# Reordering the instruction lists of five engines in a fused adaLN attention and feed-forward block on one core

## The chip, the cores and the metric

The kernel runs on one core of a Trainium2 chip. A core has five engines with an instruction list of their own: TensorE (PE, whose weight loads the profile shows as PEld), VectorE (DVE), ScalarE (ACT), GpSimd (POOL) and SyncE (SP, which here only issues transfers). An engine takes its list in order, and the lists meet only at semaphores. The metric is the device time of one execution in microseconds (us), as the median of several runs; one further execution was profiled.

## The reference

For each of 32 samples `x` is 256 rows of 128 numbers. What is computed, cut to what matters here:

```python
h = layernorm(x) * (1 + ca) + sa
Q, K, V = h @ wq, h @ wk, h @ wv                      # 16 heads of 8
local = window_attention(Q, K, V)                     # window 32, the block and the one before
GQ, GK, GV = h @ wgq, pool(h @ wgk), pool(h @ wgv)    # 8 heads, 64 latents, pooled over 4 rows
rem = softmax(mask(GQ @ GK.T / sqrt(8))) @ GV @ r_out_w
gl, gr = sigmoid(sum(Q * gate_local_w)), sigmoid(sum(Q * gate_remote_w))
x = x + ga * ((gl * local + gr * rem) @ w_out)
h = layernorm(x) * (1 + cb) + sb
x = x + gb * ffn(h)                                   # weights mixed per sample from the mean of relu(h @ w1.T + b1)
```

Everything is float32.

## The kernel before

**Stages.** After a set-up, 36 steps run the attention part as a software pipeline (`pipeline`), then four groups of eight samples run the feed-forward part. In step `it` five samples are in work at once: the first norm of sample `it`; projections, scores and softmax numerators of `it-1`; value products, gating and remote part of `it-2`; the output projection of `it-3`; the second norm and the hidden layer of the mixing gate of `it-4`. Steps 0 to 3 and 32 to 35 are written out, 4 to 31 are a hardware loop. Each engine has a `step(it)` that says in which order it takes the pieces; this order is written by hand, and it is what the change edits.

**Banks.** PSUM has eight banks: `SB[0..3]` hold the window scores of four head groups, then their transposed probabilities; `WB[0..3]` hold projections, latent scores, latent values, the gates, and the output products. `bank_free` makes TensorE wait until the last reader of a bank is done.

**One step, before the change.** TensorE: `projections` (wk and wq in L835 and L836, wgq and wgk in L839 and L840, wv in L847, the two gate products in L855 from `gate_w` and `hT`), `latent_T`, `probs_T` for all four groups (L896), `latent_values` (L946), `latent_value_rows` (L957), output projection (L987), transposes of the second norm (L994), `values` (L927, row sums in L931, into `SB[2]`), remote product (L1001), hidden layer (L1011, into `SB[1]`), transposes of the first norm (L1018), both `latent_scores` (L970), `scores` (L871 to L882). VectorE: both norms' statistics (L546, L551), `xn_a` (L555), latent denominators (`rlden` L615, `rem_n` L618), `GVBD` (L624), `y_ga` (L591), local denominators (`rden` L634, `a_loc` L636), pooling `hpT` (L640), the gating (L647, L649), then maxima and subtractions of the latent scores (L576, L582) and of the window scores (L561, L568). ScalarE: copies of `K_ch`, `QT`, `GQT`, `GKT`, `V_rows` (L411 to L426) with the exponentials of `probs` (L403) among them, `PL` (L435, L438), the four `PT` copies (L443), `xn_d` (L449), `h2T` (L452), relu (L456), `hT` (L464), exponentials of the latent scores (L470), tanh of the gates (L475). GpSimd: `KM` (L336, the keys spread over head groups), `inv_std` of the first norm (`ve_a` L327, `rstd_a` L329), the second norm's four small operations (L344 to L350), two halves of `PT_sum` (L358), `GKBD` (L364, the pooled keys spread over heads), `x_all` (L370), `attT` (L377). After steps 1, 2, 3 and 32 GpSimd also issues four expert-weight transfers (`load_experts`, L319 and L321). SyncE loads the next sample, stores `V_rows` and fetches it back as `VBD` when `pv_done` says that the last `VBD` has been read.

**Set-up of the gates.** After step 0 TensorE transposes wq (L1062), multiplies it by the gate columns (L1065), and ScalarE spreads the result into `gate_w` (L485); the gates are then products with `hT`.

The waits that set the order in the TensorE list look like this (L857 on, before the scores):

```python
pe.wait_ge(qt_ready, b + 1)
pe.wait_ge(km_ready, b + 1)
bank_free(pe, it, (0, hT_ready, 1, 1), (4, h2T_ready, 1, 1))
```

Of the kernel before, what the change touches and what calls it, by code (L numbers as in the profile page):

```python
# [13 lines left out]
P = 128  # L14
# [10 lines left out]
def adaln_block(nc, ins, out):  # L25
# [17 lines left out]
    with ExitStack() as ctx:  # L43
# [3 lines left out]
        def sem(name):  # L47
# [15 lines left out]
        tri, tri4, w_out, wqT, wv_in, gate_cols = (early[:, k, :] for k in range(6))  # L63
# [88 lines left out]
         silu_ready, siluT_done, siluT_ready, mod_done, mod_ready, ga_ready, ga_stored, ga_loaded, wqT_done,  # L152
         wqT_ready, attn_w_ready, gate_w_done, gate_w_ready, masks_ready, wT_done, wT_ready) = (sem(n) for n in (
             "mod_loaded", "attn_loaded", "w_loaded", "tw_loaded", "x_loaded", "mask_ready", "zeros_ready",
             "head_ready", "silu_exp", "silu_ready", "siluT_done", "siluT_ready", "mod_done", "mod_ready",
             "ga_ready", "ga_stored", "ga_loaded", "wqT_done", "wqT_ready", "attn_w_ready", "gate_w_done",
             "gate_w_ready", "masks_ready", "wT_done", "wT_ready"))
# [144 lines left out]
        def _(pool):  # L302
# [28 lines left out]
            def step(it):  # L331
# [6 lines left out]
                if has(it, 0):  # L338
                    inv_std(it, aggr_a, mv_a, ve_a, eps_a, rstd_a, rstd_a_s)
                if has(it, 4):  # L340
# [9 lines left out]
                    nc.gpsimd.tensor_tensor(shift_d[:], neg_d[:], rstd_d[:], ALU.mult).then_inc(shift_ready, 1)  # L350
                if has(it, 2):

                    b = it - 2
                    both = PT[:, 0:G * 2 * S].rearrange("p (g k s) -> p g k s", g=G, k=2)
                    for i in range(2):
                        pool.wait_ge(pt_copied, 4 * b + 2 * (i + 1))
                        pair = slice(2 * i, 2 * i + 2)
                        nc.gpsimd.tensor_tensor(PT_sum[:, pair, :], both[:, pair, 0, :], both[:, pair, 1, :], ALU.add  # L358
                                                ).then_inc(pts_ready, 1)
                if has(it, 1):  # L360

                    b = it - 1
                    pool.wait_ge(gq_ready, 2 * (b + 1))
                    nc.gpsimd.tensor_tensor(GKBD[0:NL], bc(GKT[:], [NL, LH, NL], 1),  # L364
                                            bc(head[0:NL, 0:LH], [NL, LH, NL], 2), ALU.mult).then_inc(gkbd_ready, 1)
# [29 lines left out]
        def _(act):  # L395
# [8 lines left out]

            def step(it):
                if has(it, 1):
# [4 lines left out]
                    nc.scalar.copy(K_ch[:], WB[0][:, S:2 * S]).then_inc(k_ready, 1)  # L411
                    nc.scalar.copy(QT[:], WB[0][:, 0:S]).then_inc(qt_ready, 1)
                if has(it, 2):
                    probs(it - 2, 1)
                if has(it, 1):
                    act.wait_ge(gqk_done, b + 1)
                    nc.scalar.activation(GQT[0:NL], WB[1][0:NL, 0:S], ACT.Copy, scale=SCALE / POOL).then_inc(gq_ready, 1)
                    nc.scalar.copy(GKT[:], WB[1][0:NL, S:S + NL]).then_inc(gq_ready, 1)
                if has(it, 2):
                    probs(it - 2, 2)  # L420
# [6 lines left out]
                if has(it, 2):  # L427
                    probs(it - 2, 3)
                if has(it, 2):
                    b = it - 2  # L430
                    if isinstance(it, int) and it == 2:
                        act.wait_ge(ga_stored, 16)

                    act.wait_ge(lpt_done, 2 * b + 1)
                    nc.scalar.copy(PL[:, :, 0:S].rearrange("p g (t s) -> p t g s", t=T),  # L435
                                   WB[0][:].rearrange("p (t g s) -> p t g s", t=T, g=LG)).then_inc(lpt_copied, 1)
                    act.wait_ge(lpt_done, 2 * b + 2)
                    nc.scalar.copy(PL[:, :, S:S + P],  # L438
                                   WB[1][:, 0:2 * P].rearrange("p (g s) -> p g s", g=LG)).then_inc(lpt_copied, 1)
                    for q in range(4):  # L440

                        act.wait_ge(pt_done, 4 * b + (q + 1))
                        nc.scalar.copy(PT[:, q * 2 * S:(q + 1) * 2 * S], SB[q][:]).then_inc(pt_copied, 1)  # L443
                if has(it, 4):
# [6 lines left out]
                    act.wait_ge(x2T_done, b + 1)  # L451
                    nc.scalar.activation(h2T[:, bass.ds(b * S, S)], SB[0][:, 0:S], ACT.Identity,  # L452
                                         scale=cb1T[:, bass.ds(b, 1)], bias=sbT[:, bass.ds(b, 1)]).then_inc(h2T_ready, 1)
                    act.wait_ge(hid_done, b + 1)

                    nc.scalar.activation(SB[1][:, 0:S], SB[1][:, 0:S], ACT.Relu, bias=gate_b1[:],  # L456
                                         accum_out=hsum[:, bass.ds(b, 1)]).then_inc(hid_summed, 1)
                if has(it, 0):
# [5 lines left out]
                    nc.scalar.activation(hT[:], SB[0][:, 0:S], ACT.Identity, scale=ca1T[:, bass.ds(it, 1)],  # L464
                                         bias=saT[:, bass.ds(it, 1)]).then_inc(hT_ready, 1)
                if has(it, 1):
                    b = it - 1
                    for t, pl in ((0, PlA), (1, PlB)):
                        act.wait_ge(ls_sub, 2 * b + (t + 1))
                        nc.scalar.activation(pl[:], pl[:], ACT.Exp).then_inc(pl_ready, 1)  # L470

# [5 lines left out]
                    probs(b, 0)  # L477

            def after(it):
                if it == 0:  # L480
                    act.wait_ge(wqT_done, 1)
                    nc.scalar.copy(wqT, SB[1][:, 0:D]).then_inc(wqT_ready, 1)
                    act.wait_ge(gate_w_done, 1)
                    for k in range(2):
                        nc.scalar.copy(gate_w[:, k, :].rearrange("p (h d) -> p h d", d=HD),  # L485
                                       bc(SB[2][:, k * H:(k + 1) * H], [P, H, HD], 2)).then_inc(gate_w_ready, 1)
# [24 lines left out]
        def _(dve):  # L511
# [83 lines left out]
            def step(it):  # L595
# [3 lines left out]
                if has(it, 0):  # L599
                    dve.wait_ge(x_loaded, 16 * (it + 1))  # L600
                    stats(x_all[:, bass.ds(it * S, S)], st_a, stat_a, mv_a, aggr_a, it)
# [3 lines left out]
                if has(it, 0):  # L605
                    dve.wait_ge(rstd_a_s, it + 1)
                    at_least(dve, xT_done, it)
                    normed(x_all[:, bass.ds(it * S, S)], mv_a, rstd_a, xn_a, xn_a_s)
                    if isinstance(it, int) and it == 0:
                        modulation()  # L610
# [8 lines left out]
                if has(it, 1):  # L619

# [7 lines left out]
                if has(it, 3) and not tail:  # L628
                    output_times_ga(it - 3)
                if has(it, 2):  # L630
# [3 lines left out]
                    nc.vector.reciprocal(rden[:], SB[2][:, S:2 * S]).then_inc(rden_ready, 1)  # L634
                    dve.wait_ge(rden_ready, b + 1)
                    nc.vector.tensor_tensor(a_loc[:], SB[2][:, 0:S], rden[:], ALU.mult).then_inc(a_ready, 1)  # L636
                if has(it, 0):

                    dve.wait_ge(hT_ready, it + 1)
                    nc.vector.tensor_reduce(hpT[:], hT[:].rearrange("p (n k) -> p n k", k=POOL), AX.X, ALU.add  # L640
                                            ).then_inc(hp_ready, 1)
                if has(it, 2):
                    b = it - 2
                    dve.wait_ge(a_ready, b + 1)
# [493 lines left out]
```

## Time and profile before

| what | us |
|---|---|
| median of 3 runs | 749.49 |
| lowest and highest run | 747.51, 749.99 |
| profiled execution, its device time | 748.97 |
| profiled execution, span from first to last instruction | 747.2 |
| busy in the span: PE, DVE, ACT, POOL | 645.6, 538.1, 384.9, 294.9 |
| granted TensorE clock, mean over the span | 0.979 |

The profiled execution took 748.97 us, 1.77 us more than its span and 0.52 us less than the median. In the timeline a row gives the start, the duration, the engine, the line, what is written from what, and in square brackets how long the engine had been idle and what ended that. Rows of the same group of instructions are merged, with their count. Step 2 begins with the projections at 34.86, step 32 at 524.93; the feed-forward groups fill the time from about 575.

### The profile page before, as it was taken

Reading aid. Unit: us, or ns where it says so; the run is one execution under the profiler, and the core shown is the slowest. Engines: PE = TensorE matmul, PEld = TensorE weight load, DVE = VectorE, ACT = ScalarE, POOL = GpSimd, SP = SyncE. Lnnn points to the kernel's source line nnn. Section 1 sums busy time; section 2 is a strip of 40 time slices with the busy share of each in tenths; the row PEclk is TensorE's granted clock in tenths of the full one; section 3 lists DMA queues with packets and bytes.
Section 4 is the critical chain, followed back from the end, with each engine's and each line's share of the span. In section 5 each row is a group of like instructions: output and inputs, shape, how many; then the busy total and the mean of one; then the engine's idle time right before and its main releaser. Section 6 shows DMA issues by size and latency. Waiting matters only on the chain.

```text
span 747.2 us, 24120 instructions
## 1 busy us (share of the span) xinstructions
PE 645.6 (86%) x8822; PEld 506.4 (68%) x8822; DVE 538.1 (72%) x1241; ACT 384.9 (52%) x910; POOL 294.9 (39%) x415
## 2 busy tenths in 40 slices
PE   5588888788888878888887888888779999999998
PEld 3366666566666656666665666666558999898996
DVE  5568788888878888887888888788755546273552
ACT  2256655666665566666555666655543223423233
POOL 2256555455555545555554555555530000000000
PEclk9699999999999999999999999999978999999999
DMA  3757111000101100010110001010140010100101
GB/s 99 174 78 96 32 24 32 21 21 21 28 22 24 31 21 21 21 28 21 24 32 21 21 21 28 21 24 18 29 44 0 10 35 15 32 24 21 34 9 49
DMA packets 65797, 24.84 MB, mean 33 GB/s; under 512 B 38440, under 2 KB 64360, under 8 KB 65648
## 3 DMA queue, kind: packets, MB, share of 16 engines
q1 hardware_dynamic: 64320, 18.25, 10.2%
q0 software_dynamic: 1456, 6.31, 5.6%
q8 instruction: 14, 0.23, 0.1%
q14 instruction: 7, 0.06, 0.0%
HBM read 16.13 MB, written 8.40 MB: 33 GB/s over the span
## 4 chain that ended last, share of the span: by engine, by line
PE 42%; DVE 26%; ACT 15%; issue 14%; POOL 1%; ACTq 1%; DVEq 1%; DMA 0%; SPq 0%; POOLq 0%
DVE mx L561 10%; PE SB L820 7%; PE WB L808 7%; DVE rden L634 5%; ACT PT L443 5%; PE SB L927 5%; PE WB L795 4%; PE SB L795 4%; ACT xn_d L449 4%; DVE Pr L568 3%; ACT Pr L403 3%; PE SB L882 2%; PE SB L931 2%; ACT PL L435 2%; PE WB L970 2%
## 5 line engine op out<-in xcount | busy, mean ns | idle before, releaser
L336 POOL TENSOR_TENSOR KM<-K_ch,bd_scale 128x1024 f32<-128x1024 f32 x32 | 60.6, 1893 | 125.2 <-ACT K_ch L411 125.2
L634 DVE RECIPROCAL rden<-SB 128x256 f32<-128x256 f32 x32 | 56.2, 1758 | 54.5 <-PE SB L931 54.5
L506 ACT ACTIVATE Pr<-WB,mb1T 128x256 f32<-128x256 f32 x128 | 49.8, 477 | 75.7 <-PE WB L808 75.6
L561 DVE TENSOR_REDUCE mx<-SB 128x8 f32<-128x512 f32 x128 | 87.2, 681 | 1.5 <-PE SB L882 1.5
L403 ACT ACTIVATE Pr<-Pr 128x512 f32<-128x512 f32 x128 | 80.8, 631 | 10.8 <-DVE Pr L568 7.2
L568 DVE TENSOR_TENSOR Pr<-SB,mx 128x512 f32<-128x512 f32 x128 | 84.6, 681 | 0.0
L358 POOL TENSOR_TENSOR PT_sum<-PT 128x512 f32<-128x512 f32 x64 | 80.3, 1275 | 3.8 <-ACT PT L443 3.8
L443 ACT COPY PT<-SB 128x512 f32<-128x512 f32 x128 | 66.1, 622 | 0.0
L896 PE MATMUL SB<-ident,Pr 128*128 128x128 f32 x512 | 63.0, 276 | 0.9 <-ACT Pr L403 0.9
L820 PE MATMUL SB<-Pr,GA 128*128 128x256 f32 x256 | 61.2, 381 | 0.0
L835 PE MATMUL WB<-hT,wk 128*128 128x256 f32 x64 | 23.3, 448 | 43.2 <-DVE PlB L582 43.2
L808 PE MATMUL WB<-h2T,mW 128*128 (+1 forms) x256 | 60.2, 380 | 0.0
L896 PEld LDWEIGHTS SB<-ident,Pr 128*128 128x128 f32 x512 | 57.8, 143 | 1.8 <-ACT Pr L403 1.8
L377 POOL TENSOR_TENSOR attT<-a_gated,rem_g 128x256 f32<-128x256 f32 x32 | 23.2, 725 | 88.8 <-DVE a_gated L647 85.7
L470 ACT ACTIVATE PlA<-PlA 128x256 f32<-128x256 f32 x32 | 13.3, 416 | 79.5 <-DVE PlA L582 79.5
L808 PEld LDWEIGHTS WB<-h2T,mW 128*128 128x128 f32 x256 | 48.2, 190 | 6.4
L820 PEld LDWEIGHTS SB<-Pr,GA 128*128 128x128 f32 x256 | 46.1, 190 | 6.2 <-DVE GA L675 1.2
L835 PEld LDWEIGHTS WB<-hT,wk 128*128 128x128 f32 x64 | 10.0, 196 | 57.7 <-DVE PlB L582 53.7
L882 PE MATMUL SB<-KM,QT 32*32 32x256 f32 x2048 | 48.4, 387 | 0.0
L970 PE MATMUL WB<-GKBD,GQT 128*128 128x512 f32 (+1 forms) x128 | 47.9, 498 | 0.0
L456 ACT ACTIVATE SB<-SB,gate_b 128x256 f32<-128x256 f32 x32 | 14.3, 448 | 63.8 <-PE SB L1011 63.8
L615 DVE RECIPROCAL rlden<-WB 128x128 f32<-128x128 f32 x32 | 30.7, 958 | 19.7 <-PE WB L946 19.7
(195 smaller groups left out, 1518.5 us busy)
## 6 DMA issues: line engine op xcount, KB each, us to landing
x_all<-in_L_attn_x SPq DMA_DIRECT2D x32, 128.0 KB, 2.1
v_rows<-V_rows SPq DMA_DIRECT2D x32, 128.0 KB, 1.8
VBD<-v_rows SPq DMA_DIRECT2D x128, 32.0 KB, 1.8
TW<-in_L_ffn_TW POOLq DMA_DIRECT2D x16, 256.0 KB, 9.5
GA<-ga_rows POOLq DMA_DIRECT2D x1, 2048.0 KB, 10.5
out_x<-attT SPq DMA_DIRECT2D x16, 128.0 KB, 1.8
out_x<-y_ga SPq DMA_DIRECT2D x16, 128.0 KB, 1.8
PT<-in_L_ffn_W SPq DMA_DIRECT2D x2, 256.0 KB
```

What stands on the lines that cost most here:

```text
L336: nc.gpsimd.tensor_tensor(KM[:, :, W:KW], bc(K_ch[:], [P, 4, S], 1), bc(bd_scale[:], [P, 4, S], 2), ALU.mult).then_inc(km_ready, 1)
L358: nc.gpsimd.tensor_tensor(PT_sum[:, pair, :], both[:, pair, 0, :], both[:, pair, 1, :], ALU.add).then_inc(pts_ready, 1)
L403: nc.scalar.activation(Pr[:, k, :], Pr[:, k, :], ACT.Exp).then_inc(p_ready, 1)
L443: nc.scalar.copy(PT[:, q * 2 * S:(q + 1) * 2 * S], SB[q][:]).then_inc(pt_copied, 1)
L561: nc.vector.tensor_reduce(mx[:, k, :], SB[k][:].rearrange("p (h j) -> p h j", h=8), AX.X, ALU.max).then_inc(mx_ready, 1)
L568: nc.vector.tensor_tensor(Pr[:, k, :].rearrange("p (w h c) -> p h w c", w=2, h=8), SB[k][:].rearrange("p (h w c) -> p h w c", w=2, h=8), b ...
L634: nc.vector.reciprocal(rden[:], SB[2][:, S:2 * S]).then_inc(rden_ready, 1)
L808: last = mm(WB[2 * (j % 2) + c // 2][:, (c % 2) * S:(c % 2 + 1) * S], mW1[:, j, c * P:(c + 1) * P], h2T[:, bass.ds((g * GB + j) * S, S)], ...
L820: last = mm(SB[j % 2][:, 0:S], mW2[:, c, j, :], u[j % 2][:, c, :], start=(c == 0), stop=(c == FC - 1))
L882: last = mm(SB[g][W * q:W * q + W, 4 * HALF * t:4 * HALF * (t + 1)].rearrange("p (h j) -> p h j", h=4), QT[rows, W * blk:W * blk + W], KM[ ...
L896: last = nc.tensor.transpose(SB[q][:, k * P:(k + 1) * P], Pr[:, q, o:o + P], ident[:])
L970: mm(WB[1 - t][:, 0:8 * m].rearrange("p (h j) -> p h j", h=8), GQT[:, t * P:(t + 1) * P], GKBD[:, :, 0:m], start=True, stop=True).then_inc ...
```

## The change

TensorE: `probs_T` is split into two and two; the first latent score product stands before the second half of them, the second one before the norms' transposes; both norms' transposes stand before `latent_value_rows` and `values`; `scores` follows `values` directly; the remote product, the gates and the hidden layer come last. `latent_value_rows` now waits for the subtraction of the first latent tile (`PlA`), whose scores share its bank. The gates are products of `gate_w` with `QT` instead of `hT`, and wait for `a_ready`, since `values` now writes `WB[2]`, the gates' bank. The first norm's transposes go to `SB[1]`, the hidden layer to `SB[0]`, and waits for `s_sub` (first window group subtracted).

VectorE: statistics of the second norm first, then of the first; latent denominators; maxima and subtractions of the latent scores around `xn_a`; then `hpT`, `GVBD`, `rden`, `a_loc`; the first window group's maximum and subtraction; the gating; the other three groups.

ScalarE: the projections' copies first, the `PT` copies spread out (0, 1, 2, 3) with exponentials, `V_rows` and `xn_d` among them, `hT` right after the last copy, relu and tanh last.

GpSimd: `GKBD` right behind `KM`; the second norm before `inv_std`; then `PT_sum`.

Set-up: `gate_w` is made by VectorE in two products of `head` and `gate_col`; the transpose, the product, the copies and their semaphores are gone. SyncE is unchanged.

The core of the diff; pieces that only change their place are named in words:

```diff
@@ gpsimd step
                     nc.gpsimd.tensor_tensor(KM[:, :, W:KW], bc(K_ch[:], [P, 4, S], 1), bc(bd_scale[:], [P, 4, S], 2), ALU.mult
                                             ).then_inc(km_ready, 1)
-                if has(it, 0):
-                    inv_std(it, aggr_a, mv_a, ve_a, eps_a, rstd_a, rstd_a_s)
+                    pool.wait_ge(gq_ready, 2 * (b + 1))
+                    nc.gpsimd.tensor_tensor(GKBD[0:NL], bc(GKT[:], [NL, LH, NL], 1), bc(head[0:NL, 0:LH], [NL, LH, NL], 2), ALU.mult).then_inc(gkbd_ready, 1)
                 if has(it, 4):
...
                     nc.gpsimd.tensor_tensor(shift_d[:], neg_d[:], rstd_d[:], ALU.mult).then_inc(shift_ready, 1)
+                if has(it, 0):
+                    inv_std(it, aggr_a, mv_a, ve_a, eps_a, rstd_a, rstd_a_s)
                 if has(it, 2):
...
-                if has(it, 1):
-                    pool.wait_ge(gq_ready, 2 * (b + 1))
-                    nc.gpsimd.tensor_tensor(GKBD[0:NL], bc(GKT[:], [NL, LH, NL], 1), bc(head[0:NL, 0:LH], [NL, LH, NL], 2), ALU.mult).then_inc(gkbd_ready, 1)
@@ scalar step, new order of the part after GKT
+                    probs(b, 1)
                     PL copies
+                    probs_copy(b, 0)
+                    probs(b, 2)
+                    probs(b, 3)
+                    probs_copy(b, 1)
                     V_rows copy
+                    probs_copy(it - 2, 2)
                     xn_d
+                    probs_copy(it - 2, 3)
+                    hT
+                    latent_exp(it - 1, 0, PlA)
+                    h2T
+                    latent_exp(it - 1, 1, PlB)
+                    probs(it - 1, 0)
+                    relu
+                    tanh of the gates
@@ vector step, new order
+                    stats of the second norm, stats of the first norm
                     rlden, rem_n
+                    latent_maximum(it - 1, 0, W)
                     normed(x_all[...], mv_a, rstd_a, xn_a, xn_a_s)
+                    latent_lowered(it - 1, *latent_tiles[0])
+                    latent_maximum(it - 1, 1, NL)
                     output_times_ga(it - 3)
+                    latent_lowered(it - 1, *latent_tiles[1])
                     hpT
                     GVBD
-                    nc.vector.reciprocal(rden[:], SB[2][:, S:2 * S]).then_inc(rden_ready, 1)
+                    nc.vector.reciprocal(rden[:], WB[2][:, S:2 * S]).then_inc(rden_ready, 1)
                     a_loc
+                    maximum(b, 0)
+                    lowered(b, 0)
                     rem_g, a_gated
+                    maximum(b, 1)
+                    maximum(b, 2)
+                    lowered(b, 1)
+                    maximum(b, 3)
+                    lowered(b, 2)
+                    lowered(b, 3)
@@ tensor
-                for k in range(2):
-                    last = mm(WB[2][:, k * S:(k + 1) * S], gate_w[:, k, :], hT[:], start=True, stop=True)
+            def gates(it):
+                bank_free(pe, it, (2, a_ready, 1, 1))
+                for k in range(2):
+                    last = mm(WB[2][:, k * S:(k + 1) * S], gate_w[:, k, :], QT[:], start=True, stop=True)
+                last.then_inc(gates_done, 1)
@@ tensor, latent_value_rows
-                bank_free(pe, it, (2, lpt_copied, 2, 2), (1, gq_ready, 2, 2))
+                pe.wait_ge(ls_sub, 2 * b + 1)
@@ tensor step, new order
                     projections(it)
                     latent_T(it)
+                    probs_T(it, 0)
+                    probs_T(it, 1)
                     latent_values(it)
+                    latent_scores(it, 0, W)
+                    probs_T(it, 2)
+                    probs_T(it, 3)
                     output projection
+                    latent_scores(it, 1, NL)
                     transposes of xn_d
+                    transposes of xn_a
+                    latent_value_rows(it)
                     values(it)
+                    scores(it)
                     remote product
+                    gates(it)
+                    bank_free(pe, it, (1, s_sub, 4, 1))
                     hidden layer
@@ tensor, after(0)
-                    nc.tensor.transpose(SB[1][:, 0:D], wq[:], ident[:]).then_inc(wqT_done, 1)
-                    mm(SB[2][:, 0:2 * H], wqT, gate_cols[:, 0:2 * H], start=True, stop=True).then_inc(gate_w_done, 1)
```

## Rows read from the trace of the kernel before

**Rows 1.** Busy time of each engine in eleven steps of the loop (windows view).
```profile
core 0: us, PE busy (x) PEld busy (x) DVE busy (x) ACT busy (x) POOL busy (x), PEclk, DMA share, GB/s
312.26:492.06 179.80, 153.65 (x2640) 113.74 (x2640) 149.59 (x364) 111.74 (x264) 96.79 (x132) 1.00 0.10 24
```

**Rows 2.** Timeline of PE: the projections' first product in steps 2, 19 and 32.
```profile
34.86 1.22 PE L835 MATMUL WB<-hT,wk 128*128 128x256 f32 x2
...
312.26 0.70 PE L835 MATMUL WB<-hT,wk 128*128 128x256 f32 x2 [1.44 <-DVE PlB L582]
...
524.93 0.67 PE L835 MATMUL WB<-hT,wk 128*128 128x256 f32 x2 [1.51 <-DVE PlB L582]
```

**Rows 3.** Waits of PE and DVE in the same eleven steps: total, times, longest.
```profile
PE WB L835 <- DVE PlB L582: 15.9, 11, 1.5
PE SB L994 <- ACT xn_d L449: 9.7, 11, 0.9
...
DVE rden L634 <- PE SB L931: 19.3, 11, 1.8
```

**Rows 4.** Timeline of PE and ACT: wq, the copy of K_ch, and xn_d of one step.
```profile
312.80 0.59 PE L836 MATMUL WB<-hT,wq 128*128 128x256 f32 x2
...
313.98 0.35 ACT L411 COPY K_ch<-WB 128x256 f32<-128x256 f32 x1
...
319.79 0.93 ACT L449 ACTIVATE xn_d<-x_all,shift_d,rstd_d 128x128 f32 x2
```

**Rows 5.** Timeline of POOL in one step (KM is of the next step).
```profile
300.81 0.20 POOL L327 TENSOR_TENSOR ve_a<-mv_a,eps_row 128x2 f32<-128x2 f32 x1 [0.86 <-DVE mv_a L551]
...
301.75 0.20 POOL L344 TENSOR_TENSOR ve_d<-mv_d,eps_row 128x2 f32<-128x2 f32 x1
...
302.96 2.51 POOL L358 TENSOR_TENSOR PT_sum<-PT 128x512 f32<-128x512 f32 x2
305.43 1.04 POOL L364 TENSOR_TENSOR GKBD<-GKT,head 64x512 f32<-64x512 f32 x1
...
314.41 1.89 POOL L336 TENSOR_TENSOR KM<-K_ch,bd_scale 128x1024 f32<-128x1024 f32 x1 [3.80 <-ACT K_ch L411]
```

**Rows 6.** Timeline of step 1: GpSimd and VectorE side by side, a transfer's issue.
```profile
21.55 1.03 POOL L364 TENSOR_TENSOR GKBD<-GKT,head 64x512 f32<-64x512 f32 x1
21.61 1.31 DVE L555 TENSOR_SCALAR xn_a<-x_all,mv_a,rstd_a 128x128 f32<-128x128 f32 x2 [1.08 <-POOL rstd_a L329]
...
25.42 0.66 POOL L319 DMA_DIRECT2D TW<-in_L_ffn_TW  x1
```

**Rows 7.** Timeline of DVE in one step of the loop.
```profile
301.82 0.61 DVE L555 TENSOR_SCALAR xn_a<-x_all,mv_a,rstd_a 128x128 f32 x2 [0.33 <-POOL rstd_a L329]
...
302.84 0.96 DVE L615 RECIPROCAL rlden<-WB 128x128 f32<-128x128 f32 x1 [0.41 <-PE WB L946]
...
303.92 0.29 DVE L618 TENSOR_TENSOR rem_n<-WB,rlden 128x128 f32<-128x128 f32 x1
...
306.49 1.76 DVE L634 RECIPROCAL rden<-SB 128x256 f32<-128x256 f32 x1 [1.75 <-PE SB L931]
...
308.28 0.42 DVE L636 TENSOR_TENSOR a_loc<-SB,rden 128x256 f32<-128x256 f32 x1
...
310.60 0.41 DVE L582 TENSOR_TENSOR PlA<-WB,lmx 128x256 f32<-128x256 f32 x1
...
310.93 0.68 DVE L561 TENSOR_REDUCE mx<-SB 128x8 f32<-128x512 f32 x1
```

**Rows 8.** Timeline of PE: latent value rows in step 1; values, hidden layer, transposes in the loop.
```profile
18.69 0.32 PE L957 MATMUL WB<-wgv,hpT 128*32 128x16 f32 x16
...
304.79 1.20 PE L927 MATMUL SB<-PT,VBD 128*32 128x64 f32 x64
...
306.90 0.60 PE L1011 MATMUL SB<-h2T,gate_w1T 128*128 x2
...
307.34 0.38 PE L1018 MATMUL SB<-ident,xn_a 128*128 128x128 f32 x2
```

**Rows 9.** Timeline of PE in the set-up: the gate columns' product.
```profile
12.96 0.61 PE L1065 MATMUL SB<-Pr 128*128 128x32 f32 x2 [1.48 <-DVE w_out_half L712]
```

More of the change, by code:

```diff
@@ L62, in adaln_block @@
         early = Pr[:].rearrange("p k n -> p (k n)").rearrange("p (k n) -> p k n", n=P)
-        tri, tri4, w_out, wqT, wv_in, gate_cols = (early[:, k, :] for k in range(6))
+        tri, tri4, w_out, wv_in = (early[:, k, :] for k in range(4))
         c_rows, silu_a, silu_b, silu_c, ga_sign, ga_abs = (early[0:B, k, :] for k in range(6, 12))
@@ L427, in step @@
                 if has(it, 2):
[L428 to L443, printed above, removed]
+                    probs_copy(it - 2, 2)
                 if has(it, 4):
@@ L450, in step @@
                                              scale=rstd_d[:, t:t + 1], bias=shift_d[:, t:t + 1]).then_inc(xn_d_s, 1)
[L451 to L457, printed above, removed]
+                if has(it, 2):
+                    probs_copy(it - 2, 3)
                 if has(it, 0):
@@ L605, in step @@
                 if has(it, 0):
[L606 to L610, printed above, removed]
+                    dve.wait_ge(x_loaded, 16 * (it + 1))
+                    stats(x_all[:, bass.ds(it * S, S)], st_a, stat_a, mv_a, aggr_a, it)
                 if has(it, 2):
@@ L633, in step @@
                     dve.wait_ge(pv_done, b + 2)
-                    nc.vector.reciprocal(rden[:], SB[2][:, S:2 * S]).then_inc(rden_ready, 1)
+                    nc.vector.reciprocal(rden[:], WB[2][:, S:2 * S]).then_inc(rden_ready, 1)
                     dve.wait_ge(rden_ready, b + 1)
[L636 to L641, printed above, removed]
+                    nc.vector.tensor_tensor(a_loc[:], WB[2][:, 0:S], rden[:], ALU.mult).then_inc(a_ready, 1)
@@ L656, in step @@
-                    latent_lowered(b, *latent_tiles[0])
-                    maximum(b, 0)
-                    latent_lowered(b, *latent_tiles[1])
-                    for k in range(4):
-                        if k < 3:
-                            maximum(b, k + 1)
-                        lowered(b, k)
+                    maximum(b, 1)
[4 more added lines that the diff above has]
+                    lowered(b, 3)
@@ L848, in projections @@
                 last.then_inc(v_done, 1)
-                bank_free(pe, it, (2, tg_ready, 1, 1))
-                if isinstance(it, int) and it == 1:
-                    pe.wait_ge(ga_ready, 1)
-                    pe.wait_ge(gate_w_ready, 2)
-                for k in range(2):
-                    last = mm(WB[2][:, k * S:(k + 1) * S], gate_w[:, k, :], hT[:], start=True, stop=True)
-                last.then_inc(gates_done, 1)
             def scores(it):
@@ L930, in values @@
                 for g in range(G):
-                    last = mm(SB[2][W * g:W * g + W, S:2 * S], ones_bd[:], PT_sum[:, g, :], start=False, stop=True,
+                    last = mm(WB[2][W * g:W * g + W, S:2 * S], ones_bd[:], PT_sum[:, g, :], start=False, stop=True,
                               skip_group_check=True)
@@ L995, in step @@
                     last.then_inc(x2T_done, 1)
+                if has(it, 0):
+                    pe.wait_ge(xn_a_s, T * (it + 1))
+                    bank_free(pe, it, (2, pt_copied, 4, 2), (1, hT_ready, 1, 1))
+                    for t in range(T):
+                        last = nc.tensor.transpose(SB[1][:, t * P:(t + 1) * P], xn_a[:, t, :], ident[:])
+                    last.then_inc(xT_done, 1)
+                if has(it, 1):
+                    latent_value_rows(it)
                 if has(it, 2):
                     values(it)
+                if has(it, 1):
+                    scores(it)
+                if has(it, 2):
                     pe.wait_ge(remn_ready, it - 2 + 1)
@@ L1009, in step @@
                     pe.wait_ge(h2T_ready, b + 1)
-                    bank_free(pe, it, (2, pt_copied, 4, 2), (5, hid_summed, 1, 1))
-                    mm(SB[1][:, 0:S], gate_w1T[:], h2T[:, bass.ds(b * S, S)], start=True, stop=True
+                    bank_free(pe, it, (1, s_sub, 4, 1))
+                    mm(SB[0][:, 0:S], gate_w1T[:], h2T[:, bass.ds(b * S, S)], start=True, stop=True
                        ).then_inc(hid_done, 1)
-                if has(it, 0):
-                    pe.wait_ge(xn_a_s, T * (it + 1))
-                    bank_free(pe, it, (4, h2T_ready, 1, 1), (2, pt_copied, 4, 1), (1, hT_ready, 1, 1))
-                    for t in range(T):
-                        last = nc.tensor.transpose(SB[0][:, t * P:(t + 1) * P], xn_a[:, t, :], ident[:])
-                    last.then_inc(xT_done, 1)
-                if has(it, 1):
-                    latent_scores(it)
-                    scores(it)
             def experts(g0, g1, ready):
```

169 lines of the change are left out of this document (99 added, 70 removed).

## The prediction

> **What bounds the kernel now.** I began with the busy time of the engines in eleven steps of the loop [rows 1]: divided by 11 it is 13.97 us a step for TensorE, 13.60 for VectorE, 10.16 for ScalarE and 8.80 for GpSimd. The projections' first product starts at 34.86 in step 2 and at 524.93 in step 32 [rows 2], so a step takes 490.07 / 30 = 16.34 us. No engine is full. The reader is to see that two of them are within 2.8 us of it, so an order that lets them run side by side has up to 2.3 us a step to win, and no more.
>
> The waits view says where TensorE's 2.3 us are [rows 3]: 1.45 a step before the projections, until VectorE has subtracted `PlB`, and 0.88 before the second norm's transposes, until ScalarE has come through its copies to `xn_d`. VectorE in its turn waits 1.75 a step for the row sums of `values`. The engines hand one baton around: VectorE's subtractions, ScalarE's copies, TensorE's `values`, VectorE's reciprocal `rden` and all the maxima behind it. That round is the bound, and the change cuts it up.
>
> **The change, part by part.** Removed are both TensorE waits. `hT` of the next sample is made before `values`, so the projections can follow the hidden layer at once, and the first window group's subtraction frees what TensorE needs at the end of a step. What is late next is found by following the new lists from the start of wk (time 0) until wk starts again. GpSimd now has all its early work in a row (KM, GKBD, second norm, first norm), and `xn_a`, now ahead of `values`, hangs on its end. The sum along that path:
>
> - wk and wq end at 312.80 + 0.59 - 312.26 = 1.13 [rows 2, 4]. A hand-off between engines is 0.08 (K_ch ends at 314.33, KM starts at 314.41 [rows 4, 5]); K_ch takes 0.35 and a second hand-off follows, so KM starts at 1.64. Relu and tanh stand ahead of K_ch on ScalarE. The hidden layer ends 0.16 into the step (it starts 0.44 before wk and lasts 0.60, see the last bullet), which leaves them 1 us; I cost them at nothing, and up to 0.2 a step if they run over.
> - KM 1.89 and GKBD 1.04 [rows 5]: 4.57. The second norm takes 302.96 - 301.75 = 1.21, the first 301.75 - 300.81 = 0.94, each to the start of the next GpSimd instruction [rows 5]: 6.72. Statistics are done by then, as VectorE begins the step with them.
> - Behind the first norm GpSimd takes `PT_sum` at once, half of 2.51 [rows 5]. Step 1 shows what this does: `xn_a` was issued 0.06 after GKBD and its two tiles took 1.31 instead of 0.61, ending at 22.92, or 0.34 after GKBD's end at 22.58 [rows 6, 7]. While GpSimd ran a long operation VectorE's `xn_a` stood still. So the first half ends at 6.72 + 1.26 = 7.98 and `xn_a` at 8.32. In the loop before the change only the second norm's tiny operations follow, and 0.61 is kept.
> - `PlA` is queued behind `xn_a` on VectorE, 0.41 [rows 7]: 8.73. `latent_value_rows` now waits for it: a hand-off and 0.32 [rows 8] give 9.13. Its cost was shared with `latent_values` before; alone it lies between nothing and 0.32, and I take the row.
> - `values` starts there. From its first product to `rden` are 306.49 - 304.79 = 1.70 [rows 7, 8]: 10.83. `rden` to `a_loc` 1.79 and `a_loc` 0.42 [rows 7]: 13.04.
> - The first window group: maximum 0.68, a gap of 0.12 for a result that the next VectorE instruction needs (303.92 against 302.84 + 0.96), subtraction taken as equal, 0.68 [rows 7]: 14.52. `scores` fits in the 2.2 us of `rden` and `a_loc`; the gates, four products as before, fit beside the maximum.
> - The hidden layer waits for that subtraction, and wk stands behind it: a hand-off and 307.34 - 306.90 = 0.44 [rows 8] give 15.04.
>
> A step of 15.04 saves 1.30, over the 30 starts from step 2 to step 32 39.0 us. TensorE and VectorE are filled to 93% and 90% by it, so nothing else is longer. The other moved waits are costed at nothing. The first latent scores wait for GKBD, with TensorE's whole list behind them, but the path runs over GpSimd anyway. `VBD` is fetched by SyncE after `pv_done`, at about 10.8, and needed at 9.1 of the next step, 13 us later. `V_rows` is copied later, and its store only feeds that fetch.
>
> Two terms lie outside the loop. **Set-up:** the gate columns' product had 1.48 of waiting and 0.61 of its own [rows 9], both in front of the first projections; VectorE gains two products of 128x128, 0.29 each by the size of `rem_n` [rows 7]. Between nothing and 2.1 saved, I take 1.5. **Transfer issues:** after steps 2 and 3 GpSimd issues four expert transfers, up to 0.66 each [rows 6], 2.6 in all. Before, KM waited 3.80 for K_ch [rows 5], which hid them. Now `attT` comes after the first subtraction and two gating operations: 14.52 + 0.42 + 0.42 + 0.08 + 0.63 = 16.07 (the gating as long as `a_loc`; `attT` half as long as a half of `PT_sum`, by its width), and the issues reach to 18.7, against 15.04 + 1.64 = 16.68 for KM. That is 2.0 twice, 4.0 us lost; the bounds are 0 and 5.2.
>
> Sum: 748.97 - 39.0 - 1.5 + 4.0 = 712.5 for an execution like the profiled one, which stood 0.5 below the median of the runs; I give 712.5, rounded to 712.
>
> **The rivals.** *The port is no obstacle.* If `PT_sum`'s first half starts late (its second `PT` copy missing) or lets `xn_a` through, `xn_a` ends at 6.72 + 0.08 + 0.61 = 7.41 instead of 8.32, a step is 14.13, just above TensorE's own 13.97, and the time 748.97 - 66.3 + 2.5 = 685. For it speaks that 0.61 holds in the loop now [rows 7]; against it, that the one case with a long operation behind the first norm shows the stall [rows 6].
>
> *The halves and the tiles alternate (slower).* `xn_a` is two instructions and `PT_sum` too. The second half waits for the last `PT` copy. ScalarE's list from K_ch to that copy holds the same instructions that took it from 313.98 to 319.79 + 0.93, 6.74 us [rows 4], so the copy ends at 1.21 + 6.74 = 7.95, against 7.98 for the end of the first half: a toss. If it is earlier, the second half can go between the two tiles. Then `xn_a` ends 1.26 + 0.34 = 1.60 later, a step is 16.64, above the 16.34 of now, and the time 748.97 + 9.0 + 2.5 = 760. It decides from the moment that the copy ends before the first tile is through. For it speaks the closeness of the two times; against it, that in step 1 the second tile followed the first without a break [rows 6], though no other GpSimd computation was queued there.
>
> The Trainium skill, page "SBUF — State Buffer", section "Who interferes with whom", says that VectorE and GpSimd share one pair of ports, that an instruction that needs it holds it to its end while the other blocks, and that the order of issue decides. The trace agrees for one GpSimd operation. By that rule a second half issued before the second tile goes first, which is this rival; no run here shows two of each.
>
> *Both halves first (no change).* If GpSimd keeps the port across both, `xn_a` ends 1.26 later, a step is 16.30 and the time 748.97 - 1.2 + 2.5 = 750. For it speaks that the halves follow each other without a gap when both copies are there (2.51 for two [rows 5]); against it, again the 7.95.
>
> *TensorE stalls a little more.* With some 40 waits in a step and TensorE 93% full, 0.4 a step more puts the time at 712.5 + 12 = 724.
>
> **How the numbers follow.** The forecast gets 0.5: every term but one is a row, and the port's stall is seen. The free port gets 0.2, since a delay of 1 us on ScalarE would bring it about. The alternation gets 0.1, both halves first 0.1, the extra stalls 0.1. A measurement of this kernel can tell about 0.3% (2.2 us) from no change. Faster is forecast, free port, extra stalls and a bit of the no-change case, 0.82; the same is 0.07, the rest of that case; slower 0.11, the alternation with the edge of the other. The range takes in the free port with its set-up bound (683) and goes up past the extra stalls to 740, where a small part of the two bad cases is reached; it leaves out most of these. The likeliest case alone spans 703 to 722: 0.3 a step either way.
>
> **What would show it.** Right: a step of about 15.0; `xn_a` pairs at 1.5 instead of 0.61; the wait of the projections for `PlB` gone; KM starting less than 1 us after `attT` in the loop; VectorE's wait for `rden` under 0.5. Free port: `xn_a` stays at 0.61 and TensorE's busy time fills its step to 98%. Alternation: the pair takes over 2.5, with the second half of `PT_sum` between. Wrong: TensorE idle by a us or more ahead of anything but `latent_value_rows`, the first norm's transposes or the hidden layer; or a chain through ScalarE.

## The result, and the profile after

The changed kernel takes 742.19 us in the median of 13 runs (740.43 to 747.46), the kernel before 749.05: a ratio of 0.9927, with a 95% interval from 0.9905 to 0.995. It is faster, by 7 us (0.7%) and not by the 37 that were forecast. The profiled execution took 747.31 us over a span of 745.5, near the upper end of the runs.

First the starts of the projections in steps 2, 3, 4, 5 and 32 (timeline of PE of the changed kernel; wk is L847 here).

```profile
33.11 0.70 PE L847 MATMUL WB<-hT,wk 128*128 128x256 f32 x2
48.18 0.59 PE L847 MATMUL WB<-hT,wk 128*128 128x256 f32 x2
65.71 1.06 PE L847 MATMUL WB<-hT,wk 128*128 128x256 f32 x2
87.01 0.69 PE L847 MATMUL WB<-hT,wk 128*128 128x256 f32 x2
...
523.49 0.59 PE L847 MATMUL WB<-hT,wk 128*128 128x256 f32 x2
```

Step 2 starts 1.75 earlier than before [rows 2]; 1.33 of this are there when step 1's projections start (12.05 against 13.38) and come from the set-up. Step 2 takes 15.07. Steps 3 and 4 take 17.53 and 21.30, longer than any step of the loop before (16.34). The 27 steps from 5 to 31 take 436.48 / 27 = 16.17 each. So the loop gained 0.17 to 0.19 a step where 1.30 was forecast, 5 us in all, and steps 3 and 4 gave it back in this execution.

Not all of that loss is waiting. The windows view of these two steps (columns as in [rows 1]):

```profile
48.18:65.71 17.53, 14.18 (x238) 10.17 (x237) 15.06 (x32) 9.00 (x20) 10.48 (x13) 0.96 0.63 81
65.71:87.01 21.30, 17.58 (x241) 11.73 (x240) 15.25 (x34) 9.73 (x22) 10.75 (x17) 0.79 0.57 76
```

The granted clock is 0.96 and 0.79; in the loop, and in the same two steps of the kernel before, it is 1.00. It is 0.57 from 64 to 68 and 0.51 from 78 to 84, so for most of these stretches at the lower of its two levels (1.2 and 2.4 GHz). The first fall comes soon after a stop of TensorE of 1.45 us, the second in a stop of 2.24, both shown below. TensorE is busy for 17.58 us in step 4, in a step of the loop for 14.38: 3.2 of the 5.1 us by which step 4 exceeds the loop's 16.17 are products that ran more slowly.

Next a step of the loop, 313.38 to 329.55 (timelines of the changed kernel; the rows of `PT_sum` and `xn_a` are read in stretches so short that the two halves and the two tiles stand apart).

```profile
313.38 0.69 PE L847 MATMUL WB<-hT,wk 128*128 128x256 f32 x2
...
315.06 1.89 POOL L336 TENSOR_TENSOR KM<-K_ch,bd_scale 128x1024 f32<-128x1024 f32 x1 [0.95 <-ACT K_ch L417]
...
320.06 1.27 POOL L361 TENSOR_TENSOR PT_sum<-PT 128x512 f32<-128x512 f32 x1
320.13 1.28 DVE L557 TENSOR_SCALAR xn_a<-x_all,mv_a,rstd_a 128x128 f32 x1
320.74 0.57 ACT L405 COPY PT<-SB 128x512 f32<-128x512 f32 x1
321.34 1.39 DVE L557 TENSOR_SCALAR xn_a<-x_all,mv_a,rstd_a 128x128 f32 x1
321.39 1.26 POOL L361 TENSOR_TENSOR PT_sum<-PT 128x512 f32<-128x512 f32 x1
...
323.15 0.32 PE L971 MATMUL WB<-wgv,hpT 128*32 128x16 f32 x16
...
325.19 1.76 DVE L649 RECIPROCAL rden<-WB 128x256 f32<-128x256 f32 x1
```

Up to the first half of `PT_sum` everything stands where the sum put it: KM at 1.68 into the step (1.64 was worked out), the first half at 6.68 (6.72). Then the last `PT` copy ends at 321.31, the first half at 321.33. The first tile, whose row starts at 320.13, ends at 321.41, 0.08 after that half. The second half starts at 321.39, 0.08 after the copy that it needs. The second tile's row starts at 321.34, a little before that half's, and yet the tile ends 0.08 after the half, at 322.73. So `xn_a` takes 2.60 instead of 0.61 [rows 7] and ends 9.35 into the step, not at 8.32. Everything behind it is late by the same 1 us: `latent_value_rows`, `values`, `rden`, and the next wk at 16.17.

The waits of the same eleven steps (total, times, longest) show the old stalls [rows 3] gone and the new one in their place.

```profile
ACT hT L462 <- PE SB L1022: 22.7, 11, 2.1
...
PE SB L1022 <- DVE xn_a L557: 15.2, 11, 1.4
POOL KM L336 <- ACT K_ch L417: 10.5, 11, 1.0
...
PE SB L1046 <- DVE Pr L570: 4.1, 11, 0.4
```

TensorE no longer waits for `PlB` or for `xn_d`; it waits 1.38 a step for `xn_a`, ahead of the first norm's transposes (L1022), and 0.37 ahead of the hidden layer (L1046). VectorE's wait for `rden` is no longer in the list. Its busy time over these steps (windows view) is now 171.66 / 11 = 15.61 a step [rows 1: 13.60], and the 2.0 more are the two tiles standing still:

```profile
313.38:491.10 177.72, 158.16 (x2641) 112.56 (x2640) 171.66 (x364) 111.23 (x264) 97.19 (x132) 1.00 0.11 24
```

A share of 97% on VectorE would read as a full engine. It is a blocked one.

### The profile page after: what moved, and what is told of

Same layout as the page of the kernel before. It is cut to its first block and busy times, and to the rows that moved or that the text cites. A ratio compares the mean times of both kernels' runs of the same rounds, so it can differ in the third digit from the quotient of the medians.

```text
span 745.5 us, 24195 instructions
## 1 busy us (share of the span) xinstructions
PE 662.9 (89%) x8819; PEld 505.6 (68%) x8819; DVE 596.7 (80%) x1242; ACT 383.0 (51%) x907; POOL 296.1 (40%) x415
## 5 line engine op out<-in xcount | busy, mean ns | idle before, releaser
L400 ACT ACTIVATE Pr<-Pr 128x512 f32<-128x512 f32 x128 | 78.0, 640 | 119.9 <-DVE Pr L570 119.9
L557 DVE TENSOR_SCALAR xn_a<-x_all,mv_a,rstd_a 128x128 f32 (+1 forms) x64 | 76.1, 1229 | 1.4 <-POOL rstd_a L329 1.1
L405 ACT COPY PT<-SB 128x512 f32<-128x512 f32 x128 | 75.2, 590 | 2.6 <-PE SB L899 1.8
L899 PE MATMUL SB<-ident,Pr 128*128 128x128 f32 x512 | 66.8, 273 | 1.1 <-ACT Pr L400 1.0
L649 DVE RECIPROCAL rden<-WB 128x256 f32<-128x256 f32 x32 | 56.2, 1757 | 8.9 <-PE WB L935 6.8
L985 PE MATMUL WB<-GKBD,GQT 128*128 128x512 f32 (+1 forms) x128 | 56.4, 525 | 6.3 <-DVE wait_carrier L750 4.5
L462 ACT ACTIVATE hT<-SB,saT,ca1T 128x256 f32<-128x256 f32 x32 | 18.1, 566 | 70.7 <-PE SB L1022 70.7
L1022 PE MATMUL SB<-ident,xn_a 128*128 128x128 f32 x64 | 14.4, 308 | 38.8 <-DVE xn_a L557 38.8
L931 PE MATMUL WB<-PT,VBD 128*32 128x64 f32 (+1 forms) x2048 | 39.2, 228 | 3.0 <-issue 2.2
L367 POOL TENSOR_TENSOR x_all<-x_all,y_ga 128x256 f32 (+1 forms) x32 | 23.7, 741 | 43.5 <-DVE y_ga L593 43.5
```

Source lines behind the costliest of these rows:

```text
L400: nc.scalar.activation(Pr[:, k, :], Pr[:, k, :], ACT.Exp).then_inc(p_ready, 1)
L557: nc.vector.tensor_scalar(xn[:, t, :], src[:, t * D:(t + 1) * D], mv[:, t, 0:1], rstd[:, t:t + 1], ALU.subtract, ALU.mult).then_inc(xn_s, 1)
L899: last = nc.tensor.transpose(SB[q][:, k * P:(k + 1) * P], Pr[:, q, o:o + P], ident[:])
L985: mm(WB[1 - t][:, 0:8 * m].rearrange("p (h j) -> p h j", h=8), GQT[:, t * P:(t + 1) * P], GKBD[:, :, 0:m], start=True, stop=True).then_inc ...
```

## The experiments

The theory from these rows: `xn_a` and long GpSimd operations cannot run at once, and `xn_a` is now on the path; with only one half of `PT_sum` in its way a step would be the 15.04 of the forecast. One rival: TensorE's list fills about 16 us by itself. Another: `xn_a` waits for something else.

**The second half behind `xn_a`.**

```diff
                         pool.wait_ge(pt_copied, 4 * b + 2 * (i + 1))
+                        if i == 1 and has(it, 0):
+                            pool.wait_ge(xn_a_s, T * (it + 1))
```

> The changed kernel with one more wait: GpSimd takes the second half of PT_sum only when xn_a is written. Port theory (xn_a stands still while GpSimd runs both halves): the two tiles take about 1.35 us together instead of 2.60, a step 15.0 instead of 16.17, the time 742 - 28 x 1.15 = 710. Rival (TensorE's list, 14.4 us busy a step, fills the step anyway): a step stays above 15.8 and the time above 732. Rival (xn_a waits for something other than GpSimd's long operations): the tiles stay at 2.6 and the time at 742 or above.

716.31 us, ratio 0.9556 (0.9528 to 0.9583). A step takes 15.11. One step of it (timelines):

```profile
299.52 0.69 PE L849 MATMUL WB<-hT,wk 128*128 128x256 f32 x2
...
306.20 1.27 POOL L363 TENSOR_TENSOR PT_sum<-PT 128x512 f32<-128x512 f32 x1
306.27 1.54 DVE L559 TENSOR_SCALAR xn_a<-x_all,mv_a,rstd_a 128x128 f32 x2
307.96 1.29 POOL L363 TENSOR_TENSOR PT_sum<-PT 128x512 f32<-128x512 f32 x1 [0.48 <-DVE xn_a L559]
308.24 0.32 PE L973 MATMUL WB<-wgv,hpT 128*32 128x16 f32 x16
...
310.30 1.76 DVE L651 RECIPROCAL rden<-WB 128x256 f32<-128x256 f32 x1
...
314.65 0.69 PE L849 MATMUL WB<-hT,wk 128*128 128x256 f32 x2
```

One added wait makes the kernel 26 us faster. `xn_a` ends at 8.29 into the step (8.32 in the prediction), `rden` starts at 10.78 (10.83), wk at 15.13 (15.04). The TensorE rival falls: the same list now takes 15.1. The time stayed 6 above the 710: the loop has 27 steps that became 1.06 shorter, 28.6 us, where 28 of 1.15 had been expected, and the four runs spread from 713.78 to 719.98.

**Both halves behind `xn_a`** (`i == 0` in the same lines).

> The changed kernel with both halves of PT_sum behind xn_a. Port theory: the tiles take 0.61 as in the kernel before; the halves then run from about 7.5 to 10.0 us into the step and the row sums wait for them, so a step is about 15.05 and the time about 711, no better than with the second half alone behind. TensorE rival: a step above 15.8. Other-cause rival: tiles at 2.6, time at 742 or above.

717.68 us, 0.9594 (0.954 to 0.9648); a step takes 15.16 and the tiles take their usual time (0.344 the median of one). As worked out, it makes no difference whether `xn_a` waits for a half or the row sums wait for the halves.

**The last `PT` copy late, GpSimd's list untouched.** On ScalarE, copy 3 goes behind `hT`:

```diff
-                if has(it, 2):
-                    probs_copy(it - 2, 3)
                 if has(it, 0):
...
+                if has(it, 2):
+                    probs_copy(it - 2, 3)
```

> The changed kernel with ScalarE's last PT copy behind hT instead of ahead of it, and no new wait on GpSimd. If the time of the last copy decides whether the second half goes ahead of the tiles, the tiles take 1.35 together here as well; the row sums then wait for the late second half, so a step is about 16.1 and the time about 740. If GpSimd's order alone decides, the tiles stay at 2.6 and the time is above 750.

```profile
304.52 1.27 POOL L361 TENSOR_TENSOR PT_sum<-PT 128x512 f32<-128x512 f32 x1
304.59 1.53 DVE L557 TENSOR_SCALAR xn_a<-x_all,mv_a,rstd_a 128x128 f32 x2
...
307.89 1.31 POOL L361 TENSOR_TENSOR PT_sum<-PT 128x512 f32<-128x512 f32 x1 [2.10 <-ACT PT L405]
308.05 1.20 PE L931 MATMUL WB<-PT,VBD 128*32 128x64 f32 x64 [1.18 <-ACT PT L405]
```

The tiles take 1.53 together with no new wait on GpSimd (timelines, one step): what decides is whether the second half is ready when the first tile is through. The time, of a single run, was 748.77 with a step of 16.48. Worse than the 740 expected: `values` itself waits 1.18 for the late copy, ahead of the row sums.

**GpSimd's order alone, in the kernel before.** Only `GKBD` and `inv_std` are moved:

```diff
                     nc.gpsimd.tensor_tensor(KM[:, :, W:KW], bc(K_ch[:], [P, 4, S], 1), bc(bd_scale[:], [P, 4, S], 2), ALU.mult
                                             ).then_inc(km_ready, 1)
-                if has(it, 0):
-                    inv_std(it, aggr_a, mv_a, ve_a, eps_a, rstd_a, rstd_a_s)
+                    pool.wait_ge(gq_ready, 2 * (b + 1))
+                    nc.gpsimd.tensor_tensor(GKBD[0:NL], bc(GKT[:], [NL, LH, NL], 1),
+                                            bc(head[0:NL, 0:LH], [NL, LH, NL], 2), ALU.mult).then_inc(gkbd_ready, 1)
...
                     nc.gpsimd.tensor_tensor(shift_d[:], neg_d[:], rstd_d[:], ALU.mult).then_inc(shift_ready, 1)
+                if has(it, 0):
+                    inv_std(it, aggr_a, mv_a, ve_a, eps_a, rstd_a, rstd_a_s)
...
-                    pool.wait_ge(gq_ready, 2 * (b + 1))
-                    nc.gpsimd.tensor_tensor(GKBD[0:NL], bc(GKT[:], [NL, LH, NL], 1),
-                                            bc(head[0:NL, 0:LH], [NL, LH, NL], 2), ALU.mult).then_inc(gkbd_ready, 1)
```

> The kernel before, with GpSimd's list alone in the order of the change (GKBD behind KM, the second norm ahead of the first, PT_sum right behind). Port theory: xn_a takes 2.6 us here too and ends about 5.7 us later in the step than it did; VectorE reaches rden about 1.4 us later, a step is about 17.7 and the time about 790. Without a port xn_a takes 0.61, VectorE still reaches rden in time, and the time stays at 749.

799.19 us, 1.0676 (1.0655 to 1.0697), a step of 18.22. The tiles again, in the list of before (timelines):

```profile
310.23 2.51 POOL L361 TENSOR_TENSOR PT_sum<-PT 128x512 f32<-128x512 f32 x2
310.30 2.52 DVE L552 TENSOR_SCALAR xn_a<-x_all,mv_a,rstd_a 128x128 f32 x2 [2.30 <-POOL rstd_a L329]
```

This one part of the change, by itself, costs 50 us: the first norm comes later, and `xn_a` stands still beside `PT_sum`. The run does not tell the shares of the two apart, and a step is 0.5 longer than expected, which stays open. That the stall follows GpSimd's order into another kernel is the strongest evidence for it.

**Where steps 3 and 4 went.** TensorE's timeline of the changed kernel has four gaps for which the view names no releaser (with the timeline of POOL):

```profile
53.97 1.05 POOL L339 TENSOR_TENSOR GKBD<-GKT,head 64x512 f32<-64x512 f32 x1
...
55.12 0.67 PE L985 MATMUL WB<-GKBD,GQT 128*128 128x256 f32 x2 [1.81 <-issue]
63.11 0.61 PE L884 MATMUL SB<-KM,QT 32*32 32x256 f32 x2 [1.45 <-issue]
...
79.56 0.75 PE L931 MATMUL WB<-PT,VBD 128*32 128x64 f32 x18 [2.24 <-issue]
...
549.76 0.58 PE L1034 MATMUL WB<-rem_n,r_out 128*128 128x128 f32 x1 [2.52 <-issue]
```

The first is a wait all the same. It stands ahead of the first latent scores, which wait for `GKBD`; `GKBD` ends at 55.02, 0.10 before them, and it is late because GpSimd issues four transfers ahead of KM (49.72 to 52.10). The other three stand in the middle of `scores`, `values` and the remote product, where TensorE waits for nothing. They end within 14 us of the first of the four expert transfers that GpSimd issues after steps 2, 3 and 32. The kernel before issues the same transfers after the same steps, and its gaps of this kind are 0.2 us in all (TensorE's waits). The first try moved the transfers forward:

```diff
-                if 1 <= it < 4 or it == B:
-                    for e in range(2 * (it - 1), 2 * it) if it < 4 else range(6, E):
+                if it == 1 or it == B:
+                    for e in range(6) if it < 4 else range(6, E):
                         load_experts(e)
```

> The changed kernel with the expert transfers of steps 2 and 3 issued after step 1, all twelve in a row. Issue theory (four issues ahead of KM cost steps 3 and 4): KM of these steps starts within 1 us of attT, steps 3 and 4 lose their 1.8 and 5.0 us against the kernel before, the time falls by 4 to 8 us to about 736. Rival (TensorE's own gaps in steps 3 and 4, 1.8, 1.4 and 2.2 us without a releaser, come with its written-out code whatever is transferred): the gaps stay, the time falls by 2 us or less.

750.06 us, 1.0022 (1.0012 to 1.0032), 8 us worse than the changed kernel instead of 6 better. Steps 3 and 4, now without transfers, take 13.73 and 16.24, but in `scores` of step 2, where the changed kernel has no gap, there is one of 11.47 (timeline of PE):

```profile
56.41 1.11 PE L884 MATMUL SB<-KM,QT 32*32 32x256 f32 x16 [11.47 <-issue]
```

Steps 3 and 4 came out as the issue theory said, the time as neither did. The gaps went with the transfers, from steps 3 and 4 to step 2, and TensorE's code is the same: it is not the written-out code alone. The second try put them, four a step, in steps 5 to 8, ahead of `attT` (GpSimd's steps up to 8 are written out for it):

```diff
+                if isinstance(it, int) and 5 <= it < 9:
+                    for e in range(2 * (it - 5), 2 * (it - 4)):
+                        load_experts(e)
                 if has(it, 2):
                     b = it - 2
...
                     pool.wait_ge(ag_ready, b + 1)
```

> The changed kernel with the sixteen expert transfers issued in steps 5 to 8, ahead of attT, where GpSimd waits 4.6 us a step. Transfer theory (TensorE's own gaps in steps 3, 4 and 34 are its instructions arriving late behind the expert transfers, and the issues hold up KM): the gaps of 1.8, 1.4, 2.2 and 2.5 us go, steps 3 and 4 take no longer than the loop's 16.17, the time is 742 - 8 = 734 or below; xn_a keeps its 2.6. Rival (the gaps belong to code met for the first time): the gaps stay, only KM comes earlier, the time is 739 or above.

741.48 us, 0.9897 (0.9881 to 0.9914): no gap over 0.6 us is left, and yet no gain. Steps of 18.3 and 18.6 stand between the others, with waits of another kind (from 80 to 166: total, times, longest):

```profile
ACT V_rows L450 <- DMA VBD<-v_rows: 8.6, 4, 2.6
...
PE WB L1012 <- ACT V_rows L450: 7.9, 4, 2.4
```

`VBD`'s fetch is issued among four expert transfers and lands late; ScalarE's copy of `V_rows`, which may not overwrite what is being fetched, waits for it, and with it ScalarE's list and the output projection. The two long steps are also those in which the granted clock was 0.91, with TensorE busy for 15.8 us; the other two with such a wait, at a clock of 1.00, take 16.2 and 16.6. As to the gaps, it is not the transfers alone either: beside the loop, four a step make none over 0.6. All the long gaps stand beside or just behind transfers in steps that TensorE's list goes through for the first time, written out or in the loop's first pass. The version with the second half behind `xn_a` and the same transfers:

> The second half of PT_sum behind xn_a, and the transfers in steps 5 to 8. If the two costs are separate they add: a step of 15.1, no gaps, 716 - 8 = 708. If the gaps belong to first-met code: 714 or above.

715.74 us, 0.9539 (0.9506 to 0.9572): a step of 15.1 and the same four waits for `VBD` (8.1 in all), hence no gain over 716.31. The time lies where the expectation put first-met code, but the gaps are gone here too (0.4 us in all). The third try issues one transfer a step, in steps 4 to 19 (written out too), right behind `attT`, so that it has landed before `VBD` is fetched:

```diff
                     nc.gpsimd.tensor_tensor(attT[:], a_gated[:], rem_g[:], ALU.add).then_inc(att_ready, 1)
+                if isinstance(it, int) and 4 <= it < 20:
+                    e, k = divmod(it - 4, 2)
+                    load_half(e, k)
```

> The changed kernel with the same spread of the transfers alone. xn_a keeps its 2.6 and the step its 16.17; the gaps of TensorE in steps 3, 4 and 34 are gone and no step is late, so the time is 742 - 7 = 735. If transfers cost wherever they stand: 741.

734.09 us, 0.9802 (0.9783 to 0.9822), with the step at 16.18, no wait for `VBD` and 0.7 us of gaps in all (TensorE's waits):

```profile
PE SB L892 <- issue: 0.7, 2, 0.4
```

So the place of the transfers is worth 8 us. Three things are in this sum: KM and `GKBD` behind the issues, TensorE's gaps, and the lower clock. They do not all come in every execution. In the one of the version with both halves behind `xn_a`, whose transfers stand as in the changed kernel, `values` of step 4 has no gap and the granted clock is 1.00 in steps 3 and 4 (windows view). They take 17.39 and 16.68, 3.7 us more than two steps of its loop, where the changed kernel's take 6.5 more than two of its own. That the gaps are TensorE's instructions arriving late behind the transfers fits the runs, but it is argued from the gaps' place and size and was not measured by itself, and why the kernel before is spared stays open.

**The first norm first, and both costs taken away.** On GpSimd `inv_std` goes ahead of the second norm and `PT_sum` behind `xn_a`; on VectorE the statistics are swapped and `xn_a` stands right behind `rem_n`:

```diff
+                if has(it, 0):
+                    inv_std(it, aggr_a, mv_a, ve_a, eps_a, rstd_a, rstd_a_s)
                 if has(it, 4):
                     b = it - 4
                     at_least(pool, xn_d_s, T * b)
...
+                        if i == 0 and has(it, 0):
+                            pool.wait_ge(xn_a_s, T * (it + 1))
...
-                if has(it, 1):
-                    latent_maximum(it - 1, 0, W)
                 if has(it, 0):
                     dve.wait_ge(rstd_a_s, it + 1)
...
+                if has(it, 1):
+                    latent_maximum(it - 1, 0, W)
```

> As the last one, with both halves behind xn_a, the first norm ahead of the second on GpSimd and VectorE, and xn_a right behind rem_n. If the path runs over GpSimd's norms to xn_a: xn_a starts 0.3 us earlier than without the port and ends at 7.1 us into the step, the halves at 9.7, the row sums follow, a step is about 14.6 and the time about 694. If TensorE's list with its waits fills 15 us: no change against 708.

706.83 us, 0.9435 (0.9411 to 0.9459), with the transfers still in steps 5 to 8; a step takes 14.84, 0.3 less and not 0.5. The 694 is missed by 13, about half by the step and half by steps 6 to 9, which are late as above. With the transfers spread:

> The version with the first norm first and both halves of PT_sum behind xn_a, and one expert transfer a step in steps 4 to 19, issued behind attT, where GpSimd waits about 1 us for K_ch. If the late steps 5 to 8 of the versions with four transfers a step come from VBD's fetch queueing behind the expert transfers (ScalarE's V_rows copy waits 2 us for it), one at a time lands before the fetch starts: every step 14.9, the time 707 - 9 = 698. If any transfer beside the fetch costs the same: sixteen small losses instead of four, the time 703 to 712.

698.8 us, 0.9321 (0.9297 to 0.9344), and a step of 14.87. This version beats both kernels: 50 us under the one before, 43 under the changed one. In a stretch of its loop (windows view) TensorE is at 97%:

```profile
320.00:482.00 162.00, 157.14 (x2631) 110.81 (x2624) 149.64 (x358) 111.08 (x262) 96.40 (x132) 1.00 0.11 25
```

## Why the prediction was right and wrong

**What bounds the kernel** and **what the change removes** held: both TensorE stalls are gone, and the path runs over KM, `GKBD`, both norms and `xn_a`, with every term up to `PT_sum` within 0.04.

**The failed step** is the one on `PT_sum` and `xn_a`: "So the first half ends at 7.98 and `xn_a` at 8.32." That `xn_a` stands still was right; that both tiles slip between the halves was not. The last copy ended at 7.93 and the first half at 7.95, close to the 7.95 and 7.98 of the rival on alternation, and that rival's order is what the trace shows: half, tile, half, tile, in every step of the loop. I gave it 0.1 and the forecast 0.5, on the strength of one case in which no second GpSimd computation was waiting [rows 6]. That case could not tell the two apart, and it should not have weighed against a tie. The race was closer still than a tie of 0.03: the second half starts 0.02 before the first tile is through, and it came out the same way in all 27 steps (2.59 or 2.60 for the pair).

The rule of the Trainium skill, page "SBUF — State Buffer", section "Who interferes with whom", that an instruction which needs the shared ports holds them to its end and that the order of issue decides, is the one on which that rival rests. The trace agrees that a tile ends only 0.08 after the half in front of it; that the order of issue decides it does not show, since the second tile's row starts 0.05 before that of the second half, which goes first.

**The rival's price** failed too. It added a half and a tile, 1.26 + 0.34, as if a tile held GpSimd up for its whole 0.34. The halves take 2.59 against 2.51 [rows 5], because the second starts 0.06 after the first, behind its copy; in the kernel before with GpSimd's new order they take 2.51 beside the tiles too. So a tile costs GpSimd nothing that these rows show. With 1.26 + 0.08 in place of 0.34, `xn_a` ends at 9.32 and a step is 16.04 (16.17 measured), close to "both halves first" with its 16.30, and the sign is faster, not slower.

**The free port** came about in no run: where the changed kernel's tiles take their usual time, both halves are held back behind them. The nearest is step 32, which has no `xn_a`. From its projections at 523.49 to the next step's first product (timeline of PE of the changed kernel) it takes 14.17, and 14.13 had been worked out. But it has no first norm on GpSimd and no transposes of `xn_a` either, so the agreement may be luck.

```profile
537.66 0.38 PE L907 MATMUL WB<-ident,PlA 128*128 128x128 f32 x2
```

**The terms outside the loop.** Set-up: 1.5 forecast, 1.33 measured ahead of the first projections, 1.75 with step 1. Transfer issues: 4.0 forecast for two delays of KM of 2.0. KM starts 2.3 late in step 3 and 1.0 in step 4, and TensorE waits 1.8 for `GKBD` in step 3. But the two steps lost 6.8 against the kernel before in the profiled execution, and the place of the transfers is worth 8.1 in the medians. The missing part is TensorE's gaps of 1.45 and 2.24 and the lower clock of step 4, which the prediction did not have. "`VBD` ... needed at 9.1 of the next step" named the wrong reader: the copy of `V_rows` waits for the fetch some 3 us sooner. It cost nothing here, and most of the gain where the transfers met the fetch.

The miss of 30 us in the median is thus nearly all one term: 27 steps times 16.17 - 15.04 are 30.5 us. The profiled execution missed by 34.8 (747.31 against 712.5); steps 3 and 4, 4.8 longer than their 15.04 each and the 4.0 allowed for, make up the rest.

## What to carry to other kernels

Where VectorE and GpSimd work side by side, look for VectorE instructions whose time is several times that of their form, and at what GpSimd runs behind the instruction that released them; one wait that keeps the second of two GpSimd operations behind the short VectorE one was worth 26 us here. When two events that decide an order are predicted 0.03 apart, give both outcomes the same chance and price both from rows. A transfer that nobody waits for can still delay a fetch that somebody does, and its issue what stands behind it in the issuing engine's list: to give each large load a step of its own, in a gap of the issuing engine, was worth 8 us here. And before a late step is put down to waits, read its granted clock: here it made up 3.2 of 5.1 us.

## What had not been expected

TensorE stopped for 1.4 to 11.5 us in runs of products that wait for nothing, while large transfers were under way or a few us after they had been; with the transfers moved beside the loop no gap was over 0.6. The granted clock fell to the lower level in such a stop of 2.24 us, so that the products behind it took longer too. And a VectorE tile that waits for GpSimd is through 0.08 after the GpSimd operation ends, although it takes 0.34 alone. That most of its time goes on before the wait would explain it, but no run shows this.
